# Three drains of a double-buffered staging tile: counts moved behind the low parts

## What is computed

```python
h = relu(layernorm(x)); x = x + segment_sum(edge_weight * (g * (h @ W0))[dst], src)      # g = sigmoid(h @ Wg + bg)
h = relu(layernorm(x)); x = x + segment_sum(h[src], dst) @ W1.T + b1
h = relu(layernorm(x)); x = x + L2(h)   # messages [h[src], h[dst]] @ Wm + bm, summed by dst, then @ Wu + bu
h = relu(layernorm(x)); x = x + L3(h)   # hypergraph layer, two sums over the edges, then a batch norm and relu
```

## Time and profile before

| what | value |
|---|---|
| median of 3 runs | 2428.37 us |
| profiled execution, its span | 2425.13 us, 2423.3 us |
| TensorE matmul busy over the span | 94% |
| VectorE, ScalarE busy | 59%, 53% |
| build, about 120 to 1190 us: step of the loop | about 22 us |
| DMA of the count store, each of 49 | 1600 KB, 8.7 us from issue to landing |
| DMA transposes of the build | 194, 6.2 us from issue to landing |
| granted TensorE clock over the span | 0.986 |

### The profile page before, as it was taken

How to read it: one execution, slowest core, us unless ns; L and a number is a source line. 1 busy time by engine, 2 the same in 40 slices (tenths; PEclk the granted TensorE clock), 3 DMA queues, 4 the chain that set the end, 5 groups by cost and what they waited for, 6 DMA issues and landing times.

```text
span 2423.3 us, 72160 instructions
## 1 busy us (share of the span) xinstructions
PE 2277.8 (94%) x28726; PEld 2018.4 (83%) x28726; DVE 1436.6 (59%) x3406; ACT 1286.1 (53%) x2883; POOL 53.9 (2%) x57
## 2 busy tenths in 40 slices
PE   3689999999999998999989999999999999999997
PEld 3469899898898888898978888888888888787886
DVE  8879999998899998999653332433433112122223
ACT  3689999999899998999732222222221000011112
POOL 3500000000000000000000000000000000000000
PEclk9799999999999999999999999999999999999998
DMA  7799999999999999999999999999999999999997
GB/s 190 185 214 195 205 208 211 209 202 201 208 179 209 211 199 179 211 202 203 221 225 291 290 290 290 291 268 263 260 261 247 292 290 290 264 254 248 262 267 187
DMA packets 1521139, 567.94 MB, mean 234 GB/s; under 512 B 862390, under 2 KB 1519546, under 8 KB 1520727
## 3 DMA queue, kind: packets, MB, share of 16 engines
q1 hardware_dynamic: 1517285, 557.17, 105.6%
q0 software_dynamic: 1200, 4.10, 0.6%
q10 hardware_dynamic: 2370, 2.71, 0.4%
HBM read 257.85 MB, written 92.19 MB: 144 GB/s over the span
## 4 chain that ended last, share of the span: by engine, by line
PE 61%; SPq 17%; ACT 9%; DMA 7%; issue 3%; DVE 2%; POOLq 0%; POOL 0%; ACTq 0%; DVEq 0%
PE ps L808 33%; SPq L548 9%; SPq L498 5%; ACT stage L1400 4%; PE ps L703 3%; PE ps L762 3%; ACT stage L1381 3%; PE ps L705 3%; PE ps L704 3%; PE ps L763 3%; PE ps L764 3%; DMA wt<-stage 3%; PE ps L739 3%; DMA a_turned<-counts_by_source 2%; SPq L493 2%
## 5 line engine op out<-in xcount | busy, mean ns | idle before, releaser
L1400 ACT CAST stage<-ps 128x784 f16<-128x784 f32 x784 | 656.0, 837 | 21.2 <-PE ps L764 13.7
L808 PE MATMUL ps<-Ha,a_tiles 128*128 128x256 f16 (+1 forms) x4606 | 519.6, 273 | 1.6 <-DVE Ha L1176 1.5
L762 PE MATMUL ps<-hot_c,hot_r 128*128 128x98 f16 x3136 | 502.3, 210 | 18.7 <-DVE hot_c L1098 13.3
L808 PEld LDWEIGHTS ps<-Ha,a_tiles 128*128 128x128 f16 x4606 | 448.7, 97 | 64.5 <-DVE Ha L1176 1.9
L763 PE MATMUL ps<-hot_c,hot_r 128*128 128x98 f16 x3136 | 500.1, 210 | 0.0
L764 PE MATMUL ps<-hot_c,hot_r 128*128 128x98 f16 x3136 | 498.5, 209 | 0.0
L703 PE MATMUL ps<-g_in,wt 128*128 128x128 f16 x2401 | 422.4, 219 | 16.3 <-DMA wt<-stage 12.7
L1381 ACT CAST stage<-ps 128x392 f16<-128x392 f32 x784 | 403.7, 515 | 43.8 <-PE ps L739 39.5
L705 PE MATMUL ps<-g_in,wt 128*128 128x128 f16 x2401 | 422.8, 219 | 0.0
L704 PE MATMUL ps<-g_in,wt 128*128 128x128 f16 x2401 | 422.6, 219 | 0.0
L1098 DVE TENSOR_TENSOR hot_c<-hot_c,meta 128x1568 f16<-128x1568 f16 x392 | 379.4, 968 | 0.0
(11 more groups left out here) (202 smaller groups left out, 2341.5 us busy)
## 6 DMA issues: line engine op xcount, KB each, us to landing
a_tiles<-counts_by_source SPq DMA_DIRECT2D x147, 1600.0 KB, 14.7
counts_by_source<-stage SPq DMA_DIRECT2D x49, 1600.0 KB, 8.7
meta<-edge_groups SPq DMA_DIRECT2D x26, 128.0 KB, 2.6
gated_parts<-G SPq DMA_DIRECT2D x7, 448.0 KB, 5.3
g_in<-gated_parts SPq DMA_DIRECT2D x98, 32.0 KB, 4.4
wt<-stage SPq DMA_TRANSPOSE x194, 6.2
out_x<-X SPq DMA_DIRECT2D x12, 256.0 KB
edge_table<-tab ACTq DMA_DIRECT2D x1, 2040.0 KB, 10.7
```

The costliest lines, as they stand in the source:

```text
L762: mm(into(0), rows_, codes(0), start=v == 0, stop=True, skip_group_check=True)
L808: last = mm(ps[:, sum_bank(ph, j, c), 0:summed_cols(ph)], a_slot(ph, c, i), moving[:, i, 0:summed_cols(ph)], start=i == 0, stop=i == TILES ...
L1400: a.copy(stage[:, b, 0:2 * FULL].rearrange("p (k i) d -> p k i d", k=2)[:, :, 0:TILES, u * SET_COLS:(u + 1) * SET_COLS], of).then_inc(s("h ...
```

## The change

In `hand_on` the store of the counts is issued after the turn of the low parts instead of before it. The last step, j = 48, has no turn of low parts there, so its order stays as it was. Nothing else differs: same instructions, same sizes, same semaphores and same wait counts.

```diff
                     turn(0, "hi_done", f"hi_turned{b}")
-                    sp.dma_start(two_tiles(j), stage[:, b, 0:FULL].rearrange("p (i a) d -> p i (a d)", a=2)).then_inc(s(f"stored{b}"), 16)
                     if not (isinstance(j, int) and j == TILES - 1):
                         turn(1, "lo_done", f"lo_turned{b}")
+                    sp.dma_start(two_tiles(j), stage[:, b, 0:FULL].rearrange("p (i a) d -> p i (a d)", a=2)).then_inc(s(f"stored{b}"), 16)
```

## The result

The changed kernel takes 2441.34 us (median of 7 runs, 2436.01 to 2446.22) against 2428.75 us of the kernel before in the same comparison: a ratio of 1.0056, 95% interval 1.0041 to 1.0071, so 10 to 17 us slower. The profiled execution took 2444.25 us with a span of 2442.4 us, 2.9 us above its own median. The prediction was slower, 2439 us. In a comparison further down (counts first but last) one of twelve executions took 4427.21 us at a granted clock of 0.911; its ratio leaves that one out.

What follows compares the result with a forecast made beforehand. TensorE was taken to bound the build, at 21.52 of 21.92 us a step. 43 x 0.30 = +12.9 us, -2 at pass ends and about 0 in first steps make +10.9 on 2428.37: 2439 us, range 2410 to 2457.

Steps and rivals of the forecast that it cites:

- What bounds the kernel: Build's 43 undisturbed steps: TensorE is busy 925.5 of 942.65 us, so any DMA order could win only 17.1 us.
- The low turn: Low-part transposes on SyncE's queue: over 14.9 us after the step's high turn begins (T0) instead of 21.1; TensorE's 12.7 us wait vanishes.
- The store: Count store on SyncE's queue: issued at T0 (start of the high turn) + 15.04, landing 8.4 us later at T0 + 23.44.
- The hidden 0.29 us: Start of a step: TensorE does not see the first 0.29 us of a delay to ScalarE's first copy.
- the 20.9: From a step's delayed first copy to the next high turn: TensorE needs 21.2 us less 0.29, so 20.9.
- Only half counts: ScalarE's wait for the store ties step j+2 to step j: 44.4 us per two steps, 22.22 a step against 21.92.
- late: Rival, chance 0.06: turns of 7.4 us and a 9.4 us store land at T0 + 25.3; +53 us, 2481.
- The sum: Whole kernel: 43 steps x 0.30 = +12.9 us, -2 at loop-pass ends, about 0 in the first steps; +10.9 us.
- The start: First steps of the build: 2.7 us lost in step 2, 3.4 us won in step 3, together about 0.
- In time: Rival, chance 0.23: both transpose pairs issue in 5.94 us, the store lands before ScalarE needs it; -20.6 us, 2408.

Runs made afterwards that it cites:

- counts first but last: Count store issued ahead of both turns, except in the last step, which keeps the old order: 2431.45 us against 2425.50 of the kernel before.
- shorter turns: Changed kernel, second transposes of each turn leaving out 9 of 17 blocks from step 13 on: 2417.09 us against 2425.09 of the kernel before.
- One late parity alone: Count store after the low turn only in odd or only in even steps: 2435.64 or 2436.31 us, against 2425.57 of the kernel before.
- 12 extra blocks: Changed kernel with 12 of 50 count blocks stored once more, to a spare tensor, ahead of the store: 2493.76 us against 2425.09 of the kernel before.
- 26 extra blocks: Changed kernel with 26 of 50 count blocks stored once more, to a spare tensor, ahead of the store: 2551.52 us against 2425.57 of the kernel before.

## Why the prediction was right

*What bounds the kernel.* Right: it is TensorE's pace with small waits. The possible gain was overstated somewhat: 17.1 us was span minus busy time, and shorter turns won 9.8 us in 31 of the 43 steps, 13.6 us in all by the estimate above. The idle time contained short waits of TensorE for ScalarE too, 4.8 us in 15 places at line 739 before.

*The low turn.* Right, to a few tenths: forecast over at T0 + 14.9, measured T0 + 15.0, and the wait at line 703 gone. The held `g_in` is a poor measure of what the store takes from the queue, though. Over the build before it lasted 3.5 to 5.4 us, and where it was short the pair behind it was longer: 12.73 us for the two in the earlier trace rows (705.86 to 718.59), 12.42 us where `g_in` took 3.77 and the pair 8.61 (413.33 to 425.75). The two together are what shrinks, to 7.93 us (804.98 to 812.91).

*The store.* Right. Issue forecast at T0 + 15.04, measured 15.2; 8.4 us to landing taken, 8.3 measured; so T0 + 23.4 against 22.9 in the step shown and 23.5 by the medians.

*The hidden 0.29 us and the 20.9.* Right: from a delayed first copy to the next T0 the profile after shows 21.0 us in the step shown and 20.63 to 21.10 over the build where the clock is 1.00, against 21.20 in the undelayed step of the earlier trace rows.

*Only half counts.* Right for waits of this size: 22.22 us forecast and 22.22 by the yardstick, 22.28 over all 43 steps. That the first two agree to 0.01 is luck, for the yardstick is not that exact. One late parity alone costs nearly as much as both (10 and 12.6 us), and 12 extra blocks gave 22.88 us against 22.9 in the first 20 steps. It falls short where a wait is followed by a lowered clock of TensorE, in this case's steps with waits of some 3 us and more, though not in all of those. That was not in the prediction, and its rival "late" lacks such a term: 26 extra blocks were forecast to cost 60 us over the changed kernel and cost some 110, and by the working above about half of the difference is a landing 1 us later than assumed; the other half, an estimate, is left for the clock.

*The sum.* 43 x 0.30 = 12.9 forecast, 15.4 measured in the profiled execution; that includes one step of 26.45 us near the end (1159.70 to 1186.15), behind a store that took 9.5 us to land (1154.35 to 1163.81), with a granted clock of 0.94 over the step. Without its 4.2 us over 22.22 the others give 11.2 us, so the sum came near partly by luck. Two small terms had the wrong sign. The two steps at the ends of the passes were to spare 2 us and cost 2.3 more; why they are longer was not tried. The start was to come out even and was 1.7 us late, but the first turn already began at 123.60 instead of 120.69, before the change can act, so these two executions can't settle that term. The median, which doesn't hang on one execution, moved by 12.6 us where the sum said 10.9.

*The rivals.* "In time" failed where the prediction had doubted it: a pair of transposes right behind a pair took 7.25 us in the step shown, not 5.94. The 350 to 400 GB/s that the Trainium skill gives for contiguous transposes (DMA: Bandwidth & Descriptors, section on latency and other measured facts) were not reached by any pair in the two kernels: the shortest kept SyncE for 5.93 us for its 41 blocks of 32 KB, 227 GB/s. The earlier trace rows is also not of transposes alone, for the store is issued at 705.24 in it. The stretch up to there, and the one between the two transposes of that pair:

```profile
701.50:702.90 1.40, 1.40 (x28) 1.37 (x25) 1.35 (x3) 1.40 (x3) 0.00 (x0) 1.00 1.54 35
703.00:705.20 2.20, 2.19 (x42) 1.92 (x40) 2.20 (x4) 2.20 (x6) 0.00 (x0) 1.00 1.23 272
```

A transpose moves 272 GB/s here while it moves, but the queue is almost still for 1.4 us between the two, at 35 GB/s. A pair's time is not its bytes over a rate alone.

## What to carry to other kernels

When buffers are emptied by several transfers in one queue, the one issued last takes the lateness: give that place to the part whose next writer or reader comes last, and work out for each part the landing against the first write of the next round. A wait for a buffer of two steps ago costs only half of its lateness per step, and delaying one parity costs nearly as much as delaying both. This ends where TensorE's granted clock falls behind a wait.

## What was unexpected

- A standstill of TensorE can cost more than itself. In a step of 28.50 us with a wait of ScalarE of 4.97 us the granted clock was 0.88, in its neighbour 1.00; from the delayed copy (1108.93) to the next T0 (1131.82) it took 22.9 us instead of 20.8.
- Delays that would fit evenly into both parities can gather in one: 28.50 and 21.40 us instead of twice 22.9. The sum is 4 us worse for the pair. The changed kernel has a little of this too: 23.2 and 21.7 us from 708.19 on, 24.17 and 21.37 from 1070.34 on.
- Two DMA queues are slower than one for this mix: 7.2 against 6.2 us to landing for a transpose, 11.7 against 8.7 for the store.
- TensorE's busy time rose by 14 us for the same work, as short waits vanish in overlapping records.
- Two transposes in a row leave the queue almost still between them: 35 GB/s for 1.4 us, 272 GB/s while the second one moves.
